# In batches 0 to 2, an accumulating DMA from GpSimd in place of VectorE's last sum

## The reference, cut to what matters

```python
xn  = layernorm(x)
xz  = xn @ W_in.T                        # 256 -> 1024, halves x_inner and z
xc  = silu(causal_conv4(x_inner) + conv_b)
h_t = 0.95 * h_(t-1) + xc_t              # scan over the tokens
y   = h * (s_C @ exp(B_log).T) * silu(z) # s_C from xc @ W_x.T
r   = xn + y @ W_out.T
ssm = (r - mean(r)) * rsqrt(var(r) + eps) * ln_g + ln_b
ffn = dequant(fp6(xn)) @ dequant(fp6(W)).T + bias
out = x + ssm + ffn
```

## Time and profile before

| | |
|---|---|
| median of 3 runs | 272.82 us (272.75 to 274.34) |
| span of the profiled execution, first to last instruction | 272.2 us |
| TensorE matmul, weight load | 217.7 us (80%), 180.9 us (66%) |
| VectorE | 236.1 us (87%) |
| ScalarE | 157.8 us (58%) |
| GpSimd | 198.4 us (73%) |
| HBM traffic over the span | 40 GB/s |
| first `take` of batch 0, 1, 2, 3 | at 76.09, 135.48, 194.16, 246.68 us |

### The profile page before, as it was taken

The page is one execution under the profiler, slowest core; times in us unless marked ns, Lnnn a source line. Parts: engine busy times, 40 slices in busy tenths (PEclk is TensorE's granted clock), DMA queues, the critical chain, the costliest instruction groups (busy, mean ns, idle before and its releaser), DMA issues.

```text
span 272.2 us, 3762 instructions
## 1 busy us (share of the span) xinstructions
PE 217.7 (80%) x1252; PEld 180.9 (66%) x1252; DVE 236.1 (87%) x353; ACT 157.8 (58%) x240; POOL 198.4 (73%) x127
## 2 busy tenths in 40 slices
PE   0469959789999997786999895896999988459940
PEld 0348836467898965775898763785989667359930
DVE  4799999989998999689699999689999978785374
ACT  2797773567953456858755355759737263733540
POOL 1428999999568788986586979985697959943142
PEclk9999995979999999999799999999999999959995
DMA  7963000000000000013202000000202000001204
GB/s 234 291 189 125 1 2 0 1 0 0 2 0 1 2 0 1 2 37 117 78 2 77 0 0 0 0 0 0 77 0 77 2 0 0 0 17 64 77 0 154
DMA packets 10773, 11.12 MB, mean 41 GB/s; under 512 B 648, under 2 KB 10120, under 8 KB 10760
## 3 DMA queue, kind: packets, MB, share of 16 engines
q1 hardware_dynamic: 9488, 9.96, 11.1%
q10 hardware_dynamic: 1272, 0.99, 1.3%
HBM read 6.76 MB, written 4.19 MB: 40 GB/s over the span
## 4 chain that ended last, share of the span: by engine, by line
DVE 32%; PE 31%; issue 16%; ACT 11%; POOL 5%; DMA 2%; DVEq 1%; ACTq 0%; POOLq 0%; SPq 0%
DVE hy L1015 6%; DVE xc L986 4%; DVE nmu L1060 4%; PE slot L747 4%; PE slot L749 4%; PE slot L748 4%; PE obank L839 3%; PE obank L838 3%; PE obank L846 3%; DVE hy L1028 3%; POOL hy L407 2%; ACT xn L586 2%; PE obank L749 2%; PE obank L747 2%; PE obank L748 2%
## 5 line engine op out<-in xcount | busy, mean ns | idle before, releaser
L747 PE MATMUL slot<-xn_hi,w_in_lo 128*128 128x512 f32 x128 | 54.9, 429 | 10.2 <-DVE xd_lo L981 4.1
L399 POOL TENSOR_TENSOR xc<-xc,tap 128x1021 f32<-128x1021 f32 x16 | 46.2, 2887 | 14.9 <-DVE xc L986 14.9
L407 POOL TENSOR_TENSOR hy<-hy,sz 128x1024 f32<-128x1024 f32 x16 | 49.6, 3099 | 6.5 <-ACT sz L630 6.5
L749 PE MATMUL slot<-xn_hi,w_in_hi 128*128 128x512 f32 x128 | 53.2, 416 | 0.0
L748 PE MATMUL slot<-xn_lo,w_in_hi 128*128 128x512 f32 x128 | 53.2, 416 | 0.0
L1015 DVE TENSOR_TENSOR_SCAN hy<-decay,xc 128x1024 f32<-128x1024 f32 x16 | 44.0, 2756 | 0.0
L986 DVE SCALAR_TENSOR_TENSOR xc<-slot,cw,xc 128x1023 f32<-128x1023 f32 (+1 forms) x32 | 40.2, 1264 | 2.3 <-ACT tap L623 1.8
L747 PEld LDWEIGHTS slot<-xn_hi,w_in_lo 128*128 128x128 f32 x128 | 25.7, 201 | 21.5 <-DVE xd_lo L981 5.2
L839 PE MATMUL obank<-w_out_hi,y_hi 128*128 128x256 f32 x128 | 32.8, 287 | 0.0
L838 PE MATMUL obank<-w_out_lo,y_hi 128*128 128x256 f32 x128 | 32.6, 285 | 0.0
L749 PEld LDWEIGHTS slot<-xn_hi,w_in_hi 128*128 128x128 f32 x128 | 25.7, 200 | 6.4
(11 more groups left out here) (109 smaller groups left out, 543.0 us busy)
## 6 DMA issues: line engine op xcount, KB each, us to landing
y<-fx SPq DMA_DIRECT2D x7, 512.0 KB, 2.9
x_in<-L_attn_x SPq DMA_DIRECT2D x3, 1024.0 KB, 5.6
x_in<-L_attn_x SPq DMA_DIRECT2D x2, 512.0 KB, 4.1
rs<-L_attn_W_in SPq DMA_DIRECT2D x2, 512.0 KB, 8.9
fx<-L_attn_W_out SPq DMA_DIRECT2D x1, 512.0 KB, 11.7
y<-fx SPq DMA_DIRECT2D x2, 256.0 KB, 2.1
fx<-L_ffn_weight ACTq DMA_DIRECT2D x1, 256.0 KB, 6.8
xc<-L_attn_B_log ACTq DMA_DIRECT2D x1, 256.0 KB
```

The costliest lines, as they stand in the source:

```text
L399: pool.tensor_tensor(xc[:, c, TAPS - 1:], xc[:, c, TAPS - 1:], tap0[:, c % 2, 0:n], ALU.add).then_inc(conv_ready, 1)
L407: pool.tensor_tensor(hy[:, c, :], hy[:, c, :], sz[:, :], ALU.mult).then_inc(hsz_ready, 1)
L747: pe.matmul(dst, w_lo, m_hi, start=first, stop=False)
L749: return pe.matmul(dst, w_hi, m_hi, start=False, stop=last)
```

## The change

VectorE's sum `finish(prev, g)` goes for batches 0 to 2. SyncE stores `fx` (x plus feed-forward) as soon as the takes of the half are done. GpSimd, when that store has landed and the half is scaled, issues a DMA that adds `rs` onto the stored rows in HBM (`add_normed`). `take` of the next batch waits for that DMA before it writes `rs` again. The last batch keeps its sum on VectorE. The loop over steps 1 and 2 is written out, and all counts are constants.

```diff
@@ every engine
-        def every_step(eng, step):
-            step(-1)
-            step(0)
-            with eng.Fori(1, LAST) as s:
+        def every_step(step):
+            for s in range(-1, NB + 1):
                 step(s)
-            step(LAST)
-            step(NB)
@@ SyncE
             def store(b, g):
-                sp.wait_ge(out_ready, 2 * b + g + 1)
+                if b == LAST:
+                    sp.wait_ge(out_ready, 1)
+                else:
+                    sp.wait_ge(obank_free, 2 + NT * b + HT * (g + 1))
...
-            with sp.Fori(0, LAST) as b:
+            for b in range(LAST):
...
+            for g in range(2):
+                sp.wait_ge(added[g], 16 * LAST)
@@ GpSimd
+            @of_batch
+            def add_normed(b, g):
+                if not is_last(b):
+                    wait(pool, stored[g], 16 * (b + 2))
+                    wait(pool, scaled_ready, 2 * b + g + 1)
+                    pool.dma_start(out[b, half(g), :].rearrange("(t p) d -> p t d", p=P), rs[:, tiles(g), :],
+                                   accum_op=ALU.add).then_inc(added[g], 16)
...
                 scale_g(prev, 0)
+                add_normed(prev, 0)
                 dequantise(here, 1)
...
                 conv_tap0(nxt, 1)
+                add_normed(prev, 1)
...
                 gate(nxt, 0)
@@ VectorE
                     wait(dve, stored[t // HT], 16 * (b + 1))
+                    wait(dve, added[t // HT], 16 * b)
...
                 y_low(here, 3)
-                finish(prev, 0)
                 block_inverse(nxt, 0)
...
                 take_tile(here, 1)
-                finish(prev, 1)
```

More of the change, by code:

```diff
@@ L55, in wait @@
 def wait(eng, sem, count):
-    if isinstance(count, int) and count <= 0:
+    if count <= 0:
         return
@@ L178, in build @@
         stored = [sem(f"stored{i}") for i in range(2)]
+        added = [sem(f"added{i}") for i in range(2)]
         ident_ready = sem("ident_ready")
@@ L292, in exists @@
         def exists(b):
-            return not isinstance(b, int) or 0 <= b < NB
+            return 0 <= b < NB
         def first(b):
-            return isinstance(b, int) and b == 0
+            return b == 0
         def of_batch(op):
@@ L305, in is_last @@
         def is_last(b):
-            return isinstance(b, int) and b == LAST
+            return b == LAST
         def of_half(op):
@@ L521, in step @@
                 gate(nxt, 0)
-            every_step(pool, step)
+            every_step(step)
             rstd_2_pair(0)
@@ L722, in step @@
                 taps(nxt, 2)
-            every_step(act, step)
+            every_step(step)
             squares_pair(0)
@@ L902, in step @@
                 z_half(nxt, 3)
-            every_step(pe, step)
+            every_step(step)
         @block.vector
@@ L917, in token_stats @@
             def token_stats(b, g):
-                if isinstance(b, int) and b == 0:
+                if b == 0:
                     dve.wait_ge(in0_loaded[g], 16)
@@ L1066, in var_2 @@
                 dve.tensor_scalar(ve2[:, cols], ssq[:, cols], 1.0 / DM, LN_EPS, ALU.mult, ALU.add).then_inc(ve2_ready, 1)
[L1068 to L1072, removed]
             def finish_half(b, g):
@@ L1183, in step @@
                 take_tile(here, 1)
-                finish(prev, 1)
-            every_step(dve, step)
+            every_step(step)
             def mean_2_pair(i):
```

## The result

The changed kernel takes 287.2 us against 273.6 us for the kernel before, measured beside each other: ratio 1.049, interval 1.043 to 1.055. It is slower by 4.9%. The forecast was 270.6 us, a gain of 0.8%, in a range that ended at 276.5. The profiled execution of the changed kernel has a span of 284.3 us and took 286.2 us in all. Ratios leave out executions that took over 1.5% longer than the fastest of the same kernel.

A forecast was written before the change was run, and what follows sets the result against it. No engine was full throughout; VectorE and GpSimd hold each other up at shared ports. Terms -0.76 - 0.1 - 1.94 + 0.4 + 0.2 = -2.2 us took span 272.2 to 270.0, plus 0.6 gave 270.6 us; range 268.3 to 276.5.

The forecast's parts named there:

- The waits in front of the DMA: On GpSimd before each accumulating DMA: waits for the store and the scaling claimed free, the store starting after four takes.
- The ports in the middle of a step: Steps 1 and 2: shifted GpSimd `y_low` lets `mean_2` in earlier; second `xd_low` 0.97 us earlier per step, 1.94 us gained.
- D: Length of the accumulating DMA's issue on GpSimd: taken as 2.4 us, with 0.37 and 4.4 us as ends.
- The removed sums: Six VectorE `finish_half` sums, claimed nearly all off the path: -0.76 us at the end of step 1, -0.1 at step 2.
- The rival of 6.6 us: Step ends: the removed sums all on the path, 3 x 2.2 us, giving 266.2 us; chance 0.02.
- The loop: Steps 1 and 2 written out: branches and register counts claimed to cost nothing that shows, 0 us.
- The landing and the last take: Step 3, second half: `take(3, 4)` waits for the DMA's landing, +0.2 us (ends 0 and 1.6).
- Rival 3: GpSimd becomes the bound with D above 3, decisive from 3.4: about 275 us, or 279.6 at 4.4; chance 0.24.
- Rival 5: VectorE's two-port operations near the DMAs keep GpSimd from writing descriptors: +1 us, 271.6 us; chance 0.04.
- The clock: Step 1, 129 to 132: granted clock at 0.50, costing about 1.45 us, left as it is in the forecast.
- Time around the span: Whole kernel: median of runs, 272.8 us, taken as 0.6 us above the profiled span, so span 270.0 became 270.6 us.

The follow-up runs named there:

- the experiment: Changed kernel with SyncE issuing the store of batch 0, first half, ahead of the load of batch 3 (the store first): 282.1 us, ratio 1.024 to the kernel before.
- the levelling wait: Changed kernel with a one-column GpSimd operation and a wait for its semaphore behind each accumulating DMA: alone 280.2 us, ratio 1.017 to the kernel before.
- the version with both repairs: Changed kernel with the store ahead of the load and a one-column operation plus wait behind each accumulating DMA: 270.1 us, ratio 0.981 to the kernel before.

## Why the prediction was wrong

**The waits in front of the DMA "are free".** This is the step that failed first. It said that the store starts when its four tiles are taken. That is what the store's own wait says; it is not when SyncE comes to it. The load of batch 3 stood ahead in the same queue with a wait for the eighth take. In the kernel before the order did no harm, because the store was wanted only at 130.8, after the load. The change moved the store's condition from 130.6 (the end of the sum) to 93.8 (the fourth take), ahead of the load's, and the store went out at 119.8: the queue's order bound. Price: 10.8 us of waiting on GpSimd, 6.9 us at `xd_low`, 5.2 us net by the experiment.

**The ports in the middle of a step.** The prediction let VectorE in at the next boundary between two GpSimd operations, as the rows before the change show. After a DMA issue that rule does not hold until GpSimd has been idle once. `mean_2` waited for all three passes (5.17 us in step 2), and VectorE's `y_low` in step 3 for everything queued. The prediction's rule held one GpSimd operation to be the most that VectorE waits for, and the sum had no term for more. By the experiments this is the larger loss: 7.1 us in the changed kernel, 11.9 us once the store is in place. With a wait that restores the rule the worked pattern appears, and the gain is 0.77 and 1.03 us in the two steps against 0.97 worked out for each.

**D, the length of the issue.** Taken as 2.4 us from GpSimd's own pass; measured 1.35 us for the accumulating DMA, 0.83 for a plain one of the same size, 0.65 for 512 bytes. What pushes `dequantise` back is more: the DMA waits for the semaphore of the `scale_g` just before it (0.56 to 0.66 us), so from the end of `scale_g` to `dequantise` pass 1.9 us in step 1 and 1.6 in steps 2 and 3 with the store first, and 2.6 and 2.4 us in steps 1 and 2 with the levelling wait too, against 0.1 in the kernel before. The prediction called that semaphore free. Its D of 2.4 us was the right shift for the version with both repairs, by luck: the issue was over-sized by 1 us, the two waits were left out, and the closeness of 270.1 to 270.6 rests on that. Nor does that agreement bear out the sum term by term, since the removed sums brought more and the last take nothing.

**The removed sums.** Right that they were mostly hidden: 0.9 us worked out, 2.0 us measured with no DMA, twice as much. The rival of 6.6 us is out. At the boundary of steps 1 and 2 the lag falls from 6.3 to 5.4 us.

**The loop.** Right, ratio 0.999.

**The landing and the last take.** The prediction had the landing 2.9 to 5.8 us behind a 2.4 us issue, so 5.3 to 8.2 us after the end of `scale_g(2, 1)`; with the issue at 261.06 and the median of 6.0 us it comes 6.6 us after it (260.50), inside. `take(3, 4)` did not wait for it all the same: in the changed kernel it follows at 267.63, right behind `var_2` and with no idle time, 7.1 us after the end of `scale_g` where 6.0 had passed before. The term of 0.2 us did not come.

**Rival 3**, GpSimd as the bound, gave the right side and a time of 275 to 279.6 us, but its mechanism, an issue above 3.4 us, did not occur. **Rival 5** had VectorE keep GpSimd from writing descriptors, for at most 1 us. It was the other way round: GpSimd's issue kept VectorE out of what followed.

**The clock.** The prediction left it alone. In the changed kernel the low stretch lay at 128 to 134, under the long wait, and the clock was back at 1.00 from 135; from the second `xd_low` of step 1 to `take(1, 0)` took 7.6 us instead of 8.3. Another came at 196 to 200, at 0.59, and with it the lag grew by 1.4 us.

**Time around the span.** I put 0.6 us between span and median. In the changed kernel the profiled execution took 1.9 us more than its span, and the same with both repairs, so the span of 272.2 belongs to an execution of about 274, one of the slower ones, and not to the median of 272.8. The 2.2 us were in effect taken off that median; beside the 273.6 us measured with the changed kernel the same gain would be 271.4 us, so this error is under 1 us.

## What to carry to other kernels

When a transfer's wait is moved earlier, read the whole queue in front of it: SyncE issued the store only when the wait of the load ahead of it was over (119.8, and 94.2 with the store first), and a consumer that is moved earlier turns a harmless order into a stall. Behind a DMA issued from GpSimd, put an idle moment: a wait for a small operation's semaphore, or a place where GpSimd waits anyway; otherwise VectorE operations that need the shared port stand still for the whole dense run that follows. In these traces an instruction on four columns took 0.16 us when free; one that shows microseconds of busy time was blocked, and its end named the blocker.

## What the runs showed of the hardware

VectorE's operations that use the port shared with GpSimd were let in between two GpSimd operations in the kernel before, even where these followed each other with no idle time (`mean_2` at 123.06, 1.83 us). After a DMA issued by GpSimd, of 512 KB with or without addition or of 512 bytes, they were not, until GpSimd had been idle: `y_low` of step 3 took 7.45, 6.94 and 6.13 us in the three cases, 3.16 without a DMA, and 1.24 or 1.78 us with a wait behind the DMA. An idle time of 0.24 us was enough behind the 512 bytes, and a gap of 0.09 us, that of the wait for the one-column operation, behind the 512 KB. The Trainium skill (SBUF — State Buffer, Who interferes with whom) has the port go to whoever starts first, for the whole instruction; these runs differ from it in that the block spans several instructions after a DMA issue. Which part of GpSimd keeps the port, and why an idle moment frees it, stays open: no run looked inside it.

An accumulating DMA of 512 KB from SBUF to HBM landed 6.0 us after the start of its issue in the median (5.8 to 7.0 in the changed kernel), a plain one issued by GpSimd from the same place after 3.4 us, and SyncE's store of the same size after 3.0 us. GpSimd's issue took 1.35, 0.83 and, for 512 bytes, 0.65 us. The queue of the accumulating DMAs moved 3168 packets, that of the plain ones 864, for the same six transfers.
